# Keys and values set up dense, their block form made by transfers, the value bias as a column, and a fourth lane for the last unit

## The reference

```python
def attention(x, ctx):                       # 16 heads of 32
    q = phase_sync(heads(x @ Wq.T + bq)); k = phase_sync(heads(ctx @ Wk.T + bk))
    v = heads(ctx @ Wv.T + bv)
    a = softmax(q @ k.T / sqrt(32)) @ v      # 64 keys
    return join(a) @ Wo.T + bo

def coupled(x):                              # three cycles
    gf = global_net(x.mean(axis=1))          # 512-256-128-1
    out = x
    for _ in range(3):
        tf = coupling_net(out)               # 512-512-256-128-1, gelu
        c = 0.1 + r * (0.7 * gf + 0.3 * tf - 0.5) * 2
        out = out + c * twist(out)
    return out

x = x + attention(layernorm(x), ctx)
x = x + coupled(layernorm(x))
```

## Time and profile before

| what | us |
|---|---|
| median of 3 runs | 1366.7 |
| lowest and highest run | 1363.84, 1367.88 |
| the profiled execution | 1367.76 |
| its span, first to last instruction | 1366.0 |
| VectorE busy | 1078.6 |
| ScalarE busy | 1064.5 |
| GpSimd busy | 622.6 |

### The profile page before, as it was taken

One profiled execution on the slowest core, in us unless ns is written; L12 is line 12 of the kernel. 1 busy time (PEld: TensorE's weight loads), 2 busy tenths in 40 slices (PEclk: granted clock), 3 DMA queues, 4 the chain that ended last, 5 costly groups with the idle time before them and its releaser, 6 DMA issues.

```text
span 1366.0 us, 27848 instructions
## 1 busy us (share of the span) xinstructions
PE 1243.7 (91%) x10392; PEld 865.6 (63%) x10392; DVE 1078.6 (79%) x2125; ACT 1064.5 (78%) x1914; POOL 622.6 (46%) x491
## 2 busy tenths in 40 slices
PE   7867888989999899999999899999999899999984
PEld 5432665658666776658665676658665667657763
DVE  6996459985999679985999769985999759984465
ACT  5743767888878978888878978888878978887665
POOL 1031026571456526562455526572455526462573
PEclk9977999999999999999999999999999999999997
DMA  7466424434335434434335434534335345421001
GB/s 229 139 135 127 99 42 68 93 69 106 75 62 114 91 75 88 101 55 105 71 63 119 72 93 87 104 55 110 71 63 111 68 98 83 79 58 44 28 1 62
DMA packets 319065, 116.54 MB, mean 85 GB/s; under 512 B 301777, under 2 KB 303569, under 8 KB 316882
## 3 DMA queue, kind: packets, MB, share of 16 engines
q1 hardware_dynamic: 318930, 114.76, 40.6%
HBM read 27.58 MB, written 19.53 MB: 34 GB/s over the span
## 4 chain that ended last, share of the span: by engine, by line
PE 51%; DVE 18%; ACT 14%; issue 8%; DMA 6%; POOL 2%; SPq 1%; ACTq 0%; DVEq 0%
PE ps L369 15%; PE ps L269 10%; PE ps L384 10%; PE ps L318 4%; ACT spent L774 4%; DMA x2T<-xr 3%; PE ps L396 3%; DVE xr L1842 3%; PE ps L287 2%; DVE prob L1862 2%; ACT z L846 2%; PE ps L404 2%; DVE xoT L1889 2%; ACT z L854 2%; DVE z L1941 1%
## 5 line engine op out<-in xcount | busy, mean ns | idle before, releaser
L2871 POOL TENSOR_TENSOR h<-z,h 128x512 f16<-128x512 f32 x192 | 241.5, 1264 | 332.2 <-DVE h L1932 332.2
L369 PE MATMUL ps<-x2T,W 128*128 128x256 f16 x3072 | 351.4, 273 | 7.0 <-issue 2.7
L369 PEld LDWEIGHTS ps<-x2T,W 128*128 128x128 f16 x3072 | 297.4, 98 | 56.5 <-issue 11.8
L384 PE MATMUL ps<-h,W 128*128 128x256 f16 x2304 | 276.0, 275 | 7.7 <-POOL h L2871 6.6
L384 PEld LDWEIGHTS ps<-h,W 128*128 128x128 f16 x2304 | 224.2, 99 | 54.6 <-issue 18.1
L2864 POOL TENSOR_TENSOR prob<-prob,rc 128x512 f32<-128x512 f32 x128 | 150.2, 1196 | 161.7 <-DVE rc L1878 161.4
L318 PE MATMUL ps<-WO,xoT 128*128 128x512 f16 x768 | 181.2, 387 | 5.5 <-DVE xoT L1889 4.7
L269 PE MATMUL ps<-xoT,WQ 128*128 128x512 f16 x768 | 173.3, 379 | 4.0 <-issue 3.4
L1932 DVE CAST h<-z 128x512 f16<-128x512 f32 x192 | 101.0, 538 | 62.7 <-ACT z L846 61.6
L1842 DVE TENSOR_TENSOR xr<-ps,xr 128x512 f16<-128x512 f32 x128 | 87.8, 686 | 64.3 <-ACT xr L762 63.1
L318 PEld LDWEIGHTS ps<-WO,xoT 128*128 128x128 f16 x768 | 75.4, 99 | 95.9 <-issue 9.9
(11 more groups left out here) (129 smaller groups left out, 2047.4 us busy)
## 6 DMA issues: line engine op xcount, KB each, us to landing
xin<-x SPq DMA_DIRECT2D x16, 1024.0 KB, 5.7
out<-ot SPq DMA_DIRECT2D x64, 256.0 KB, 2.4
fac<-coup SPq DMA_DIRECT2D x192, 0.5 KB, 2.1
kv_blocks<-kv SPq DMA_DIRECT2D x7, 384.0 KB, 3.0
kvb<-kv_blocks SPq DMA_DIRECT2D x7, 384.0 KB, 3.5
pT<-pr SPq DMA_TRANSPOSE x128, 3.3
wq_s<-wq SPq DMA_DIRECT2D x1, 1024.0 KB, 5.6
wk_s<-wk SPq DMA_DIRECT2D x1, 1024.0 KB, 10.1
```

The source lines that it names most:

```text
L369: mm = e.matmul(ps[:, BANK_F + L, at * LBLK:(at + 1) * LBLK], w, v, start=(n == 0), stop=(n == 3 * C - 1))
L384: mm = e.matmul(ps[:, BANK_F + L, m * LBLK:(m + 1) * LBLK], w, v, start=(c + m + a == 0), stop=(c == C - 1 and m == C2 - 1 and a == 2))
L2871: e.tensor_tensor(h1[:, L, LO, pair(n)], z[:, L, pair(n)], h1[:, L, HI, pair(n)], ALU.subtract).then_inc(lg[L]["lo1"], 1)
```

## The change

Keys: kst holds high and low parts dense, one eviction of 128x512 for each chunk and part, low parts straight from PSUM. Values: two batches share one product of 128x512 (four products in all), vst holds them dense, columns sorted into even and odd heads. The block form is made when a batch is loaded: kblocks is cleared once, and four transfers (one per group of 32 partitions) put the keys into their places; a fifth brings the values. A store is three transfers. The bias of the values is no longer in the product: oh and ol add it as a column. The last unit, (7,1,1), gets a lane of its own. All lists are planned anew.

```diff
-            def vmul(bt):
+            def vmul(i):
...
-                to = lambda h: ps[KEYS * h:KEYS * h + KEYS, BANK_V[bt % 3], 0:D2]
                 for c in range(C):
-                    for h in range(2):
-                        e.matmul(to(h), ctx_s[:, c, bt], half(wv_s[:, c], h), start=(c == 0), stop=False)
-                for h in range(2):
-                    mm = e.matmul(to(h), ones[0:1, 0:KEYS], half(bv_s[:], h), start=False, stop=True)
+                    mm = e.matmul(ps[:, BANK_V[i % 3]], ctx_s[:, c, pair(i)].rearrange("p b n -> p (b n)"), wv_s[:, c],
+                                  start=(c == 0), stop=(c == C - 1))
...
-                e.activation(k32[:, m], ps[:, BANK_K[m]].rearrange("p (b n) -> p b n", b=B), ACT.Identity,
-                             bias=bk_col[:, m:m + 1]).then_inc(su["k_out"], 1)
-                e.wait_ge(su["k_out"], m + 1)
-                for h in range(HPC):
-                    rows = slice(DK * h, DK * h + DK)
-                    e.activation(kpart(HI)[rows, :, m, h % 2], k32[rows, m], ACT.Copy).then_inc(su["k_hi"], 1)
+                e.activation(kst[:, HI, m].rearrange("p b n -> p (b n)"), ps[:, BANK_K[m]], ACT.Identity,
+                             bias=bk_col[:, m:m + 1]).then_inc(su["k_hi"], 1)
...
+            def v_hi(i):
+                e.wait_ge(su["v_mul"], i + 1)
+                e.activation(rows_of(vst[:, i, HI]), even_odd(ps[:, BANK_V[i % 3]]), ACT.Copy).then_inc(su["v_hi"], 1)
...
-                e.activation(xoT[:, HI, c], ps[:, BANK_M + c % 2], ACT.Copy).then_inc(sg["oh"], 1)
+                e.activation(xoT[:, HI, c], ps[:, BANK_M + c % 2], ACT.Identity, bias=bv_col[:, c:c + 1]).then_inc(sg["oh"], 1)
...
-                for h in range(HPC):
-                    rows = slice(DK * h, DK * h + DK)
-                    e.wait_ge(su["k_hi"], HPC * m + h + 1)
-                    e.tensor_tensor(kpart(LO)[rows, :, m, h % 2], k32[rows, m], kpart(HI)[rows, :, m, h % 2],
-                                    ALU.subtract).then_inc(su["k_lo"], 1)
+                e.wait_ge(su["k_hi"], m + 1)
+                e.scalar_tensor_tensor(kst[:, LO, m].rearrange("p b n -> p (b n)"), ps[:, BANK_K[m]], bk_col[:, m:m + 1],
+                                       kst[:, HI, m].rearrange("p b n -> p (b n)"), ALU.add, ALU.subtract).then_inc(su["k_lo"], 1)
...
+                e.tensor_tensor(rows_of(vst[:, i, LO]), even_odd(ps[:, BANK_V[i % 3]]), rows_of(vst[:, i, HI]),
+                                ALU.subtract).then_inc(su["v_lo"], 1)
...
-                e.tensor_tensor(xoT[:, LO, c], ps[:, BANK_M + c % 2], xoT[:, HI, c], ALU.subtract).then_inc(sg["md"], 1)
+                e.scalar_tensor_tensor(xoT[:, LO, c], ps[:, BANK_M + c % 2], bv_col[:, c:c + 1], xoT[:, HI, c],
+                                       ALU.add, ALU.subtract).then_inc(sg["md"], 1)
...
+            def zero():
+                e.memset(kblocks[:], 0.0).then_inc(su["zero"], 1)
...
+                e.dma_start(k_dram[bt], kst[:, :, :, bt]).then_inc(kv_stored[bt], 16)
+                for h in range(2):
+                    e.dma_start(v_dram[bt][KEYS * h:KEYS * h + KEYS], v_from(bt, h)).then_inc(kv_stored[bt], 16)
...
+                    e.dma_start(vblocks[:], v_dram[b]).then_inc(sg["kv_loaded"], 16)
...
+                    for h in range(2):
+                        e.dma_start(vblocks[KEYS * h:KEYS * h + KEYS], v_from(0, h)).then_inc(sg["kv_loaded"], 16)
+                for h in range(HPC):
+                    rows = slice(DK * h, DK * h + DK)
+                    src = k_dram[b][rows].rearrange("p q c n -> p (q c) n") if b else kst[rows, :, :, 0].rearrange("p q c n -> p (q c) n")
+                    to = kblocks[rows].rearrange("p q c (e n) -> p (q c) e n", e=2)[:, :, h % 2]
+                    e.dma_start(to, src).then_inc(sg["kv_loaded"], 16)
...
-            return u % LANES, u // LANES
+            return (LANES, 0) if u == 4 * B - 1 else (u % LANES, u // LANES)
...
-        BANK_X, BANK_S, BANK_M, BANK_F = 0, 1, 3, 5
+        BANK_X, BANK_S, BANK_M, BANK_F = 0, 1, 3, (5, 6, 7, 3)
...
+        last_Y = pT_flat[:, 0:8 * BLK].bitcast(F32).rearrange("p (c n t) -> p c n t", c=C, n=2)
```

The lists, cut to what the prediction speaks of. TensorE's set-up and the last batch:

```diff
+            kmul(0, 0); kmul(0, 1); kmul(0, 2); kmul(0, 3)
+            vmul(0, 0); vmul(0, 1)
             q(0, 0, 0)
...
+            vmul(0, 2)
+            q(0, 0, 1)
+            vmul(0, 3)
+            q(0, 0, 2); q(0, 0, 3)
+            s(0, 0); s(0, 1); s(0, 2)
...
+            l2(7, 0, 1, 0, 1)
+            y(7, 1, 0, 3); y(7, 1, 1, 0)
+            l3(7, 0, 1, 0)
```

VectorE's (statistics of the second block behind k_lo) and SP's:

```diff
+            k_lo(0, 0); k_lo(0, 1); k_lo(0, 2); k_lo(0, 3)
             stats(0, 0, 1, 0)
...
+            load_late(0, 0); load_late(0, 2); load_late(0, 1); load_late(0, 3)
+            kv_load(0)
+            x_turn(0, 0, 1, 0); x_turn(0, 0, 1, 1); x_turn(0, 0, 1, 2)
             kv_store(0, 1)
...
+            p_turn(0, 0, 0); p_turn(0, 1, 0); p_turn(0, 0, 1); p_turn(0, 1, 1); p_turn(0, 2, 0); p_turn(0, 3, 0)
+            p_turn(0, 3, 1); p_turn(0, 2, 1)
+            kv_store(0, 4); kv_store(0, 7); kv_store(0, 6); kv_store(0, 3)
+            p_turn(0, 4, 0)
             kv_store(0, 5)
...
             load_next(0, 0)
...
+            p_turn(0, 5, 0); p_turn(0, 5, 1); p_turn(0, 4, 1); p_turn(0, 6, 0); p_turn(0, 7, 0); p_turn(0, 7, 1)
+            p_turn(0, 6, 1)
```

More of the change, by code:

```diff
@@ L154, in program @@
         su = {n: sem(n) for n in (
-            "consts", "zero_v", "zero_g", "angle", "sines", "rotation", "v_mul", "v_hi", "v_lo", "bias_mul", "bias_out", "bo_split",
-            "wk_mul", "wk_out", "k_mul", "k_out", "k_hi", "k_lo", "w_hi", "w_lo", "w_neg", "last_row", "wq_mul",
+            "consts", "zero", "angle", "sines", "rotation", "v_mul", "v_hi", "v_lo", "bias_mul", "bias_out", "bo_split",
+            "wk_mul", "wk_out", "k_mul", "k_hi", "k_lo", "w_hi", "w_lo", "w_neg", "last_row", "wq_mul",
             "wq_hi", "wq_lo", "scalars")}
@@ L1712, in vector_program @@
         def vector_program(e):
-            @first
-            def zero_v(i):
-                e.memset(kv[:, 2 * i].bitcast(F32), 0.0).then_inc(su["zero_v"], 1)
             @first
@@ L2020, in vector_program @@
             stats(0, 0, 1, 1)
             aggr(0, 0, 1, 1)
-            stats(0, 0, 1, 2); stats(0, 0, 1, 3)
-            aggr(0, 0, 1, 2); aggr(0, 0, 1, 3)
+            stats(0, 0, 1, 2)
+            aggr(0, 0, 1, 2)
+            stats(0, 0, 1, 3)
+            aggr(0, 0, 1, 3)
             var(0, 0, 1)
+            v_lo(0, 1)
             nm(0, 0, 1)
-            k_lo(0, 0); k_lo(0, 1); k_lo(0, 2)
+            w_lo(0, 0); w_lo(0, 1)
             ql(0, 0, 0)
-            k_lo(0, 3)
-            v_lo(0, 0); v_lo(0, 1); v_lo(0, 2)
@@ L2231, in vector_program @@
             stats(1, 1, 0, 1)
[L2232 removed]
+            aggr(1, 1, 0, 1)
+            pl(1, 7)
             res(1, 2)
@@ L2313, in vector_program @@
+            coef(0, 1, 1)
+            outs(0, 1, 0, 0)
+            stats(2, 0, 1, 0)
+            aggr(2, 0, 1, 0)
+            stats(2, 0, 1, 1)
+            aggr(2, 0, 1, 1)
             xl(2, 0, 0, 3)
             hi1(1, 0, 0, 0, 1)
-            aggr(2, 0, 1, 0); aggr(2, 0, 1, 1); aggr(2, 0, 1, 2); aggr(2, 0, 1, 3)
+            stats(2, 0, 1, 2)
+            aggr(2, 0, 1, 2)
+            alph(1)
+            stats(2, 0, 1, 3)
+            aggr(2, 0, 1, 3)
             var(2, 0, 1)
-            alph(1)
@@ L3149, in sync_program @@
             load("wv", wv_s[:], by_chunk(wvT))
-            load("wv", bv_s[:], row(bv))
             load_x(1)
             x_turn(0, 0, 0, 0); x_turn(0, 0, 0, 1); x_turn(0, 0, 0, 2); x_turn(0, 0, 0, 3)
-            load_late(0, 1); load_late(0, 3); load_late(0, 0); load_late(0, 2)
-            x_turn(0, 0, 1, 0)
+            load_late(0, 0); load_late(0, 2); load_late(0, 1); load_late(0, 3)
+            kv_load(0)
+            x_turn(0, 0, 1, 0); x_turn(0, 0, 1, 1); x_turn(0, 0, 1, 2)
             kv_store(0, 1)
-            kv_load(0)
```

1823 lines of the change are left out of this document (894 added, 929 removed).

## The result

The changed kernel takes 1379.7 us (median of 4 runs, 1378.9 to 1380.0), the kernel before 1365.6 on the same chip (4 runs). The ratio is 1.0101, 95% interval 1.0084 to 1.0119: slower by 1%, where 0.4% faster was forecast and the range ended at 1368. The profiled execution's span is 1378.2 us against 1366.0; these two lie 12.2 us apart and the medians 14.1, so the traces account for 12.2. One of the five executions of run 6 took 2165 us and is left out; the other four lie between 1388.9 and 1395.0.

The account below looks back on a forecast made before the run. VectorE's queue was taken to bound up to 106 us and each batch's middle third, TensorE mostly the rest. Start -6.5, bias +2, order 0, lane -1.5 gave -6.0 us: 1360.7 us predicted, range 1351 to 1368.

Parts of the forecast that it names:

- Set-up, instruction prices: Set-up: low parts of keys and values at 0.743 us each; VectorE 8.7 us less work; first maximum at 60.0 us.
- I take 6.5 us for the start: Set-up and batch 0's start: 6.5 us gained, bounds 2.5 and 12, though TensorE allows 3.8 at the first maximum.
- the start gains only what nobody takes back: Rival, batch 0: the start gains only 2.5 us, 1365.7 us in all, no measurable change; chance 0.22.
- a thinner TensorE load may bring the low level earlier: Argument for the small-start-gain rival: between 66 and 106 us, less TensorE work may lower the granted clock sooner; no size.
- They fit with 1.2 us to spare: nothing: SP's queue, batch 0: twelve store issues ahead of p_turn(0,4,0) take 6.4 us, to 101.9, before 103.10; no cost.
- possible gain, in the upper bound: Batch 0's start: load_next's new place may lose 3.18 + 3.19 us of transposes on the chain, within the bound of 12.
- 5.1 us of slack cover the 2.5: nothing: Every batch: kv_load's five issues make the coupling turns 2.5 us later; slack before the mean's second network step covers it.
- I put it at 0, with +-0.5 us a batch: Reordered loop body: a few score, h1 and residual steps move one place; 0 cost, bounds +-3 us in all.
- The bias: Attention output evictions with a bias column, 0.743 and 0.681 us: 0.3 us a batch, at most 0.5; 2 us in all.
- The fourth lane: Last unit in its own lane: starts some 10 us earlier, fourth product ends 1.5 us earlier, bounds 0 and 4.
- the split transfers cost time: Rival, SP's queue before the coupling turns, every batch: 2.5 us uncovered in each of seven, 1378 us; chance 0.08.

Follow-up runs that it names:

- run 6: Changed kernel's set-up and stores, but the kernel before's lists from batch 0's probabilities on and no lane for the last unit: 1391.0 us, 1.0174 of the kernel before.
- Run 3: Changed kernel with batch 0's query products ahead of the value products of pairs 1 to 3: ratio 1.0061 to the kernel before.
- Run 1: Changed kernel with the fifteen store issues of batches 3 to 7 moved behind the last turn of batch 0's probabilities: ratio 1.0074 to the kernel before.
- run 9: run 6 with the keys' loads from batch 1 on moved behind the fourth turn of the next batch's first block: 1374.8 us, 1.0060 of the kernel before.
- run 2: Changed kernel with the keys' loads of batches 1 to 6 moved behind the fourth turn of the next batch's first block: ratio 1.0074 to the kernel before.
- run 5: Changed kernel with the load of batch 1's second block of x behind the last two turns for batch 0's couplings: ratio 1.0055 to the kernel before.
- run 8: Dense set-up, old lists, late stores, early query products, plus the last unit's lane and the changed kernel's lists from batch 7's couplings on: 1.0139 of the kernel before.

## Why the prediction was wrong, step by step

- **Set-up, instruction prices: right.** 746 and 686 ns for the low parts (743 taken for both), 8.4 us less for VectorE (8.7), the first maximum at 60.77 us (60.0).
- **"I take 6.5 us for the start": wrong.** The rival "the start gains only what nobody takes back" came, and more: -1.5 us at the first score, nothing at the fourth. I counted when TensorE would be through and asked only who waits for the first score. The turns of x's second block also wait for the fourth query product, and that had moved back by 2.1 us behind value products that no one needed yet. And the fifth query product took 4.47 us, not 2.76, at the low level of the clock: the rival had named this ("a thinner TensorE load may bring the low level earlier"), the sum had no term for it. The sentence that made 3.8 us into 6.5 had no row under it. Run 3, with the query products earlier than they ever were, gains 5.5 us; how the loss divides between the turns and the clock is open.
- **"They fit with 1.2 us to spare: nothing": wrong, the largest miss.** Twelve issues take 8.5 us, from 94.91 to 103.41, not 6.4: the row priced issues of one form at 0.53 us, but a store of half the values takes 0.61 to 0.69 and there is a gap behind each. That error cost little: with the same twelve issues in run 6 that turn starts at 102.64 us (103.10 before), and y of batch 0 is 0.6 us later than before. What failed is what I left out behind it in the list: three more store issues and the load of x, 3.4 us, ahead of seven turns that fill the queue (the load's new place I had even counted as a possible gain, in the upper bound). Run 1, which moves all fifteen issues, gives 5.3 us for it at y of batch 0, with a scatter of 3.
- **"5.1 us of slack cover the 2.5: nothing": wrong.** The price of issue was right: 3.3 us from 625.54 to 628.80 (run 6) where one issue took 0.6; the couplings' turns then end 3.5 us later and not 2.5, as one of the twelve took 1.41 us. The slack was not right: it was read between an input and a product on TensorE, but between them stand coef, the second and the third step of the mean's network and their activations, each a hand-over. Run 6 against run 9: 4.1 us a period under the old lists. Under the new ones 0.7 to 1.1 us are left of it in batches 2 to 5, and run 2 takes them away.
- **"I put it at 0, with +-0.5 us a batch": wrong on both sides.** In the loop the new lists are worth several us a period (run 6 against the changed kernel: 159.3 us from y to y in batch 3, 155.0 in the changed one). Outside the loop they put a load of 1 MB ahead of two turns (3.9 us, run 5) and lengthen batch 7 (2.4 us). I had looked at the loop alone; those two lines stand in the part of the lists that runs once.
- **The bias: right** in its instructions (737 and 681 ns for 743 and 681). What it costs the run is not separated: in run 9, with the old lists, q to y takes 0.5 us more than before (123.3 against 122.7, mean of batches 2 to 6), the upper bound of the step, and the bias is only one candidate.
- **The fourth lane: right in mechanism, 1.5 taken, 0.5 measured** at the last unit's fourth product, and nothing shown at the end (run 8). The end of the changed kernel is 2.3 us shorter than before, which looks like the lane and isn't: run 6, with no lane, has 131.2 us there too, before 133.7. The last 46.00 us of the kernel before and the last 43 of run 6 (columns as in the earlier trace rows):

```profile
1320.00:1366.00 46.00, 23.81 (x126) 15.95 (x126) 26.23 (x66) 24.44 (x54) 19.38 (x14) 0.76 0.15 47
```

```profile
1350.00:1393.00 43.00, 21.40 (x126) 14.78 (x126) 25.99 (x66) 24.11 (x53) 19.30 (x14) 0.83 0.16 50
```

The same 126 matmuls take 2.4 us less at a granted clock of 0.83 than at 0.76. Why the clock fell less there is open.

**The rival "the split transfers cost time"** had 0.08 and a sum of 1378 us; measured were 1379.7. Its place and its mechanism are real: run 6 is that rival, and there it costs more than it said, 4.1 us and not 2.5 a batch. But in the changed kernel it is only a part: of the 12.2 us of span 7.0 are lost ahead of y of batch 0, 5.3 of them by the stores in their new order (the same mechanism in a place it didn't name), and 3.9 by the load of x. Its number was near for half the right reason. The Trainium skill, DMA: Bandwidth & Descriptors, Rules for kernel authors, speaks against such transfers because they serialise over the same engines. As advice the trace agrees; as a mechanism it doesn't show here: the four loads of 32 partitions land 2.2 us (median) after issue, the stores of half the values 2.2, and the five transfers of a load are all there 4.6 to 5.6 us after the first issue, not after 17. What is paid for is SyncE's time to issue them; transfers of 32 KB don't show whether larger ones would hold each other up.

Still open: the 2.1 us from y of batch 1 to q of batch 2. In every kernel with the new lists that stretch is 33.9 to 34.5 us, in the five with old ones 32.4 (31.75 before), with or without the keys' loads ahead of it. So some 1.5 us belong to the lists and 0.6 to what the five share with the changed kernel; which line or which term was not tried.

## What to carry to other kernels

Before you split a transfer, list every issue on its queue from the wait ahead to the next idle gap, with what stands behind it: what an added issue costs is decided by what stands behind it up to the last consumer, not by the first (the same twelve issues cost nothing measurable in one order and stood in a stage that lost 7.6 us in another). Slack read between two far ends of a chain of small hand-overs is not slack; and a transfer that no one needs soon (a store, a load of the next block) belongs behind the turns that someone waits for, never ahead of them. When a change comes with a new order, put the new code under the old order and the old place under the new code before either is judged: here the order hid a loss of 4.1 us a period and added one of 4 us of its own.

## What was not expected of the hardware

- A small transfer costs SyncE's queue nearly as much as a large one: in the changed kernel medians of 0.52 to 0.68 us for 0.5 to 128 KB and 0.58 for 1 MB, with 0.04 to 0.06 us between two as a rule; a turn 1.23 to 1.25 us, but 2.2 to 3.9 us for the second turn behind a load of 1 MB that has just been issued.
- A turn lands 3.1 to 3.2 us after its issue (medians), and 6.2 to 7.8 us after it when it is issued within 1 us behind a load of 1 MB on the same queue; the loads themselves have a median of 5.9 us. The kernel before shows the same, up to 7.6 us.
- Batch 0 runs at a granted clock of 0.71 from 66 to 106 us in the kernel before and in the changed one, and from 106 to 141 us at 0.82 before and 0.71 after, where TensorE was busy for 29.0 and 23.8 of 35 us. The later stretch lost time twice, by the wait and by slower products behind it, as the fifth query product had at 71.5 us.
